# Query stage of a linear-attention layer: one PSUM bank at a time, with its copies in halves and quarters

## The chip, the cores and the metric

The kernel runs on all 8 NeuronCores of one Trainium2 chip. The metric is the device time in microseconds (us) of the slowest core. Every core runs the same program on its own tokens; there is no traffic between cores. Each core has a matrix engine (TensorE, PE in the profile; its weight loads are PEld), a vector engine (VectorE, DVE), an activation engine (ScalarE, ACT), GpSimd (POOL) and a queue engine (SyncE, SP). TensorE writes its results into PSUM, which has 8 banks of 512 f32 columns; VectorE and ScalarE read them from there.

## What is computed

The layer is linear attention, a layer norm, a routed low-rank feed-forward part and a second layer norm. The part around the change is the attention of a query:

```python
q = hidden_states @ Wq.T + bq                 # 16 heads of 128
sq = elu_plus_one(q)                          # elu(q) + 1
kv = jnp.einsum('bhsd,bhse->bhde', sk, v)
qkv = jnp.einsum('bhsd,bhde->bhse', sq, kv)
norm = jnp.einsum('bhsd,bhd->bhs', sq, k_sum)
attn = qkv / (norm[..., None] + EPS)
x = _layernorm(x + attn @ Wo.T)
x = _layernorm(x + ffn(x))
```

The batch has 2 sequences of 8192 tokens and 2048 features. A core owns 2048 tokens of one sequence.

## The kernel before

It has three stages, one after the other.

1. **Keys and values.** 64 tiles of 128 tokens (all of the sequence): lines 281 to 323 on TensorE. The stage ends with `kvb` (the 128x128 matrices kv of 4 key heads) and `ksum_bc`.
2. **Queries.** 16 units of 128 of the core's own tokens, u = 0 to 15. This is the stage that is changed.
3. **Output projection and feed-forward.** Lines 414 to 480 on TensorE, with the weights `wo_t` in the space of the query weights `U0`.

In the query stage two PSUM tensors of 2048 f32 columns (4 banks) alternate: `psQ[0]` is `psA`, `psQ[1]` is `psB`, and unit u uses `psQ[u % 2]` three times over. For a unit TensorE does three groups:

- `q_group(u)` (line 334): 16 steps of `dc` with 4 matmuls each, one to each bank j, so all four banks are filled together and end together; then 4 bias matmuls. 68 matmuls of 512 columns. It waits until `E2` of unit u - 2 has emptied the PSUM tensor (line 340).
- `t_group(u)` (line 355): 16 transposes of 128 columns, from `sqh` into the same PSUM tensor. It waits for `sqhat0` and `sqhat1`.
- `qkv_group(u)` (line 367): 16 matmuls of 128 columns with `kvb`, again into the same PSUM tensor. It waits for `E1`, the copy of the transposes to `sqhT`.

TensorE's order is q(0), q(1), t(0), qkv(0), q(2), t(1), qkv(1), and so on. One turn is q(u), t(u - 1), qkv(u - 1).

VectorE's order in a turn, with the lines of the profile: `min0` of columns 0 to 1023 (547), then for unit u - 1 `E1` (536, the whole 2048 columns to `sqhT`) and `E2` (540, the whole 2048 columns to `sqp`), then `stt0` (552), `min1` of columns 1024 to 2047 (554), `stt1` (557), `prod` (560), `red` (561), three small operations (562, 564, 565), `sqhat0` (568) and `sqhat1` (570). `min0` waits for the end of q(u), `E1` for t(u - 1), `E2` for qkv(u - 1). ScalarE takes the exponential of each `min` (line 651) and `stt0` and `stt1` wait for it. Each operation of VectorE is followed by a wait for its own semaphore (`opq`, line 522).

`sync` stores each `sqp` to `attn_scratch` after `E2` (line 755). GpSimd loads the tokens of two units at a time (`xt_own`, line 727), each load gated by the end of q of an earlier unit (`peq_q`), and after q(15) the eight chunks of `wo_t` (line 739), two in flight at a time, since they overwrite `U0`. The first matmuls of the third stage wait for these chunks.

The dictionaries `peq_*` and `dqabs` at the head of the file hold the semaphore counts of TensorE and VectorE that those waits use.

Of the kernel before, what the change touches and what calls it, by code (L numbers as in the profile page):

```python
# [23 lines left out]
WB_CH = 8  # L24
N_P2W = WO_CH + WB_CH

peq_q, peq_T, peq_qkv = {}, {}, {}
_c = 0
for _u in range(NTC_OWN):
    _c += 1  # L30
    peq_q[_u] = _c
    if _u >= 1:
        _c += 1
        peq_T[_u - 1] = _c
        _c += 1
        peq_qkv[_u - 1] = _c
_c += 1
peq_T[NTC_OWN - 1] = _c
_c += 1
peq_qkv[NTC_OWN - 1] = _c  # L40

pe2_mm3 = {}
pe2_y1t = {}
# [33 lines left out]
def _dq_seg(u, names):  # L77
    global _cq
    for n in names:
        _cq += 1  # L80
        dqabs[(u, n)] = _cq
for _u in range(NTC_OWN):
    _dq_seg(_u, ["min0"])
    if _u >= 1:
        _dq_seg(_u - 1, ["E1", "E2"])
    _dq_seg(_u, ["stt0", "min1", "stt1", "prod", "red", "eps", "recip", "cast",
                 "sqhat0", "sqhat1"])
_dq_seg(NTC_OWN - 1, ["E1", "E2"])
DQ_TOTAL = _cq

_DSEG = {
# [65 lines left out]
def build_nc():  # L157
# [16 lines left out]
    with ExitStack() as ctx:  # L174
# [97 lines left out]
        def slab_wait(eng, g):  # L272
            s = sXTe if g % 2 == 0 else sXTo
            eng.wait_ge(s, 16 * (g // 2 + 1))

        @block.tensor
        def _(tensor):
# [53 lines left out]
            tensor.wait_ge(sWLb, 16 * 12)  # L331
            tensor.wait_ge(sFin, 5)

            def q_group(u):
                par = u % 2
                s_idx = u // 2
                toff = (u - 2 * s_idx) * 128
                slab_wait(tensor, NSLAB_ALL + s_idx)
                if u >= 2:
                    tensor.wait_ge(sDVEq, dqabs[(u - 2, "E2")])  # L340
                for dc in range(16):
                    lhs = slab[s_idx % 2][:, dc, toff:toff + 128]
                    for j in range(4):
                        tensor.matmul(psQ[par][:, j * 512:(j + 1) * 512], lhs,  # L344
                                      U0[:, dc, j * 512:(j + 1) * 512],
                                      start=(dc == 0), stop=False,
                                      skip_group_check=True)
                for j in range(4):
                    mm = tensor.matmul(psQ[par][:, j * 512:(j + 1) * 512],
                                       onesr[:, :],  # L350
                                       rowq[:, j * 512:(j + 1) * 512],
                                       start=False, stop=True, skip_group_check=True)
                mm.then_inc(sPEq, 1)

            def t_group(u):
                par = u % 2
                for h in range(16):
                    if h == 0:
                        tensor.wait_ge(sDVEq, dqabs[(u, "sqhat0")])
                    elif h == 8:  # L360
                        tensor.wait_ge(sDVEq, dqabs[(u, "sqhat1")])
                    mm = tensor.matmul(psQ[par][:, h * 128:(h + 1) * 128],
                                       sqh[:, h * 128:(h + 1) * 128], I_bf[:, :],
                                       start=True, stop=True)
                mm.then_inc(sPEq, 1)

            def qkv_group(u):
                par = u % 2
                tensor.wait_ge(sDVEq, dqabs[(u, "E1")])
                for h in range(16):  # L370
                    mm = tensor.matmul(psQ[par][:, h * 128:(h + 1) * 128],
                                       kvb_v[:, h // 4, :],
                                       sqhT[:, h * 128:(h + 1) * 128],
                                       start=True, stop=True)
                mm.then_inc(sPEq, 1)

            for u in range(NTC_OWN):
                q_group(u)
                if u >= 1:
                    t_group(u - 1)  # L380
                    qkv_group(u - 1)
            t_group(NTC_OWN - 1)
            qkv_group(NTC_OWN - 1)
# [99 lines left out]
        def _(vector):  # L483
# [47 lines left out]
            sqh3 = sqh[:, :].rearrange("p (h d) -> p h d", h=16)  # L531
            rn3 = rnbf[:, :].unsqueeze(2).broadcast_to([128, 16, 128])

            def e1e2(pw):
                vector.wait_ge(sPEq, peq_T[pw])
                opq(vector.tensor_copy(sqhT[:, :], psQ[pw % 2][:, :]))  # L536
                vector.wait_ge(sPEq, peq_qkv[pw])
                if pw >= 1:
                    vector.wait_ge(sSQW, 16 * pw)
                opq(vector.tensor_copy(sqp[pw % 2][:, :], psQ[pw % 2][:, :]))  # L540

            for u in range(NTC_OWN):
                par = u % 2
                vector.wait_ge(sPEq, peq_q[u])
                if u >= 1:
                    vector.wait_ge(sACTq, 2 * u)
                opq(vector.tensor_scalar(scr1[:, :], psQ[par][:, 0:1024], 0.0,  # L547
                                         None, ALU.min))
                if u >= 1:
                    e1e2(u - 1)  # L550
                vector.wait_ge(sACTq, 2 * u + 1)
                opq(vector.scalar_tensor_tensor(sq_p1[:, 0:1024], psQ[par][:, 0:1024],
                                                0.0, scr2[:, :], ALU.max, ALU.add))
                opq(vector.tensor_scalar(scr1[:, :], psQ[par][:, 1024:2048], 0.0,
                                         None, ALU.min))
                vector.wait_ge(sACTq, 2 * u + 2)
                opq(vector.scalar_tensor_tensor(sq_p1[:, 1024:2048],
                                                psQ[par][:, 1024:2048],
                                                0.0, scr2[:, :], ALU.max, ALU.add))
                opq(vector.tensor_tensor(prod3, sq3, ks3, ALU.mult))  # L560
                opq(vector.tensor_reduce(norm16[:, :], prod3, AX.X, ALU.add))
                opq(vector.tensor_scalar(normeps[:, :], norm16[:, :], ATT_EPS,
                                         None, ALU.add))
                opq(vector.reciprocal(rnorm[:, :], normeps[:, :]))
                opq(vector.tensor_copy(rnbf[:, :], rnorm[:, :]))
                if u >= 1:
                    vector.wait_ge(sPEq, peq_T[u - 1])
                opq(vector.tensor_tensor(sqh3[:, 0:8, :], sq3[:, 0:8, :],
                                         rn3[:, 0:8, :], ALU.mult))
                opq(vector.tensor_tensor(sqh3[:, 8:16, :], sq3[:, 8:16, :],  # L570
                                         rn3[:, 8:16, :], ALU.mult))
            e1e2(NTC_OWN - 1)

            dd = [0]

# [109 lines left out]
        def _(gpsimd):  # L685
# [55 lines left out]
            gpsimd.wait_ge(sDVEq, DQ_TOTAL)  # L741
            gpsimd.wait_ge(sACTq, 2 * NTC_OWN)
            gpsimd.wait_ge(sSQW, 16 * NTC_OWN)
            gpsimd.wait_ge(sPEq, peq_T[NTC_OWN - 1])
            for i in range(4, WB_CH):
                gpsimd.dma_start(out=wbase_sb[:, 2 * i:2 * i + 2, :],
                                 in_=wb_src[:, 2 * i:2 * i + 2, :]).then_inc(sWB, 16)
# [3 lines left out]
        @block.sync  # L751
        def _(sync):
            for u in range(NTC_OWN):
                sync.wait_ge(sDVEq, dqabs[(u, "E2")])
                sync.dma_start(out=attn_dram[u], in_=sqp[u % 2][:, :]).then_inc(sSQW, 16)
            def sq_load(u):
                if u < 2:
# [69 lines left out]
```

## Time and profile before

| | us |
|---|---|
| time, median of 2 runs | 1610.43 |
| the two runs | 1610.86, 1610.00 |
| the profiled execution | 1617.76 |
| its span on the slowest core (core 1) | 1616.2 |
| spans of all 8 cores | 1587.3 to 1616.2 |
| TensorE busy on core 1 | 1380.3 (85%) |
| VectorE busy on core 1 | 658.7 (41%) |

The span runs from the first to the last instruction of a core. Start times in rows are us from the start of the span of core 1, the slowest. The key stage fills the time to about 617, the query stage runs from there to 1033, and the third stage from 1054 to the end. The mean granted clock of TensorE over the span is 0.929 of full speed on core 1 and between 0.926 and 0.931 on the others.

### The profile page before, as it was taken

The numbers are of one execution on the slowest core, as the hardware profiler recorded it, in microseconds if no ns is written. First come the engines' busy times: TensorE is split into PE (matmuls) and PEld (weight loads), VectorE is DVE, ScalarE is ACT, GpSimd is POOL, SyncE is SP. The second block draws the span as 40 slices with busy tenths as digits, with TensorE's granted clock in tenths as the row PEclk, the third lists the DMA queues.
The fourth block names the chain that finished last, engine by engine and source line by source line (L and its number), as shares of the span: only waits on it lengthen the run. The fifth ranks groups of instructions, "written<-read, shape, count | busy, mean of one in ns | idle before, by whom it ended". The sixth has DMA issues, their size and how long they took to land.

```text
span 1616.2 us, 16894 instructions; the slowest of 8 cores (1587.3 to 1616.2 us)
## 1 busy us (share of the span) xinstructions
PE 1380.3 (85%) x6808; PEld 615.5 (38%) x6808; DVE 658.7 (41%) x807; ACT 123.1 (8%) x210; POOL 68.8 (4%) x75
## 2 busy tenths in 40 slices
PE   0599999999999988787787877079999999999985
PEld 0244334443444433333333333024444444444432
DVE  0122222222222222656565565424555455545533
ACT  0000000000000000001000010000100010001000
POOL 1000000101000000000000000010000000000000
PEclk9999999999999997788888878589999999999997
DMA  7577875777746523314342021991222113212201
GB/s 111 48 74 82 90 93 78 95 110 93 94 53 71 60 27 52 52 41 78 65 79 52 14 53 27 224 195 49 66 95 101 65 66 102 94 65 71 99 27 53
DMA packets 102894, 123.86 MB, mean 77 GB/s; under 512 B 4384, under 2 KB 86304, under 8 KB 98720
## 3 DMA queue, kind: packets, MB, share of 16 engines
q0 software_dynamic: 93600, 72.43, 34.4%
q1 hardware_dynamic: 6912, 33.56, 5.7%
q10 hardware_dynamic: 2304, 16.78, 3.0%
q8 instruction: 55, 0.90, 0.2%
q14 instruction: 23, 0.19, 0.0%
HBM read 170.02 MB, written 25.17 MB: 121 GB/s over the span
## 4 chain that ended last, share of the span: by engine, by line
PE 77%; DMA 13%; DVE 8%; issue 1%; ACT 0%; DVEq 0%; POOL 0%; POOLq 0%; ACTq 0%
PE psB L463 14%; PE psA L429 13%; PE psA L290 12%; PE psA L293 12%; PE psA L344 8%; DMA u<-xt_full 7%; PE psB L344 7%; DMA u<-wo_t 4%; DVE sqhT L536 2%; DMA sq_p<-brows 2%; PE psB L473 1%; PE psB L468 1%; DVE u L547 1%; PE psA L296 1%; DVE sq_p2b L540 1%
## 5 line engine op out<-in xcount | busy, mean ns | idle before, releaser
L290 PE MATMUL psA<-u 128*128 128x512 bf16 x1024 | 392.6, 383 | 71.3 <-DMA u<-xt_full 68.9
L293 PE MATMUL psA<-u 128*128 128x512 bf16 x1024 | 391.9, 383 | 0.0
L463 PE MATMUL psB<-u,sqhT 128*128 128x512 bf16 x1024 | 235.3, 384 | 0.0
L501 DVE TENSOR_SCALAR u<-psA 128x512 f32<-128x512 f32 x64 | 44.3, 692 | 405.1 <-PE psA L298 405.1
L290 PEld LDWEIGHTS psA<-u 128*128 128x128 bf16 x1024 | 100.8, 98 | 202.0 <-issue 90.5
L429 PE MATMUL psA<-u,sq_p 128*128 128x512 bf16 x512 | 123.2, 389 | 30.4 <-DMA u<-wo_t 27.8
L344 PE MATMUL psA<-u 128*128 128x512 bf16 x512 | 129.8, 421 | 20.9 <-DVE sq_p L540 18.2
L293 PEld LDWEIGHTS psA<-u 128*128 128x128 bf16 x1024 | 101.0, 99 | 115.7 <-issue 4.1
L463 PEld LDWEIGHTS psB<-u,sqhT 128*128 128x128 bf16 x1024 | 100.6, 99 | 115.9 <-issue 5.1
L344 PE MATMUL psB<-u 128*128 128x512 bf16 x512 | 127.6, 416 | 18.3 <-DVE sq_p2b L540 18.3
L429 PE MATMUL psA<-u,sq_p2b 128*128 128x512 bf16 x512 | 120.3, 383 | 2.8 <-DVE fpA L589 2.8
L344 PEld LDWEIGHTS psA<-u 128*128 128x128 bf16 x512 | 53.9, 106 | 96.2 <-issue 48.0
L344 PEld LDWEIGHTS psB<-u 128*128 128x128 bf16 x512 | 53.2, 105 | 90.9 <-issue 41.3
L647 ACT ACTIVATE u<-u 128x512 f32<-128x512 f32 x64 | 40.3, 629 | 559.7 <-DVE u L501 559.7
L429 PEld LDWEIGHTS psA<-u,sq_p 128*128 128x128 bf16 x512 | 49.0, 100 | 84.0 <-issue 37.3
L429 PEld LDWEIGHTS psA<-u,sq_p2b 128*128 128x128 bf16 x512 | 48.8, 99 | 54.2 <-issue 5.9
L505 DVE SCALAR_TENSOR_TENSOR u<-psA,u 128x512 bf16<-128x512 f32 x64 | 44.3, 692 | 57.7 <-ACT u L647 57.7
L651 ACT ACTIVATE u<-u 128x1024 f32<-128x1024 f32 x32 | 33.8, 1056 | 380.4 <-DVE u L547 253.1
L712 POOL DMA_DIRECT2D u<-xt_full x32 | 36.8, 1151 | 519.9 <-PE psA L298 489.0
L672 ACT CAST sqhT<-psB 128x512 bf16<-128x512 f32 x64 | 37.1, 586 | 254.4 <-PE psB L398 254.4
L618 DVE BATCH_NORM_STATS2 bnstB<-fpA 128x6 f32<-128x512 f32 x64 | 44.4, 694 | 7.0 <-DVE bnstB L618 0.5
L595 DVE BATCH_NORM_STATS2 bnstA<-fpA 128x6 f32<-128x512 f32 x64 | 44.4, 694 | 6.6
(109 smaller groups left out, 918.1 us busy)
## 6 DMA issues: line engine op xcount, KB each, us to landing
u<-xt_full POOLq DMA_DIRECT2D x32, 1024.0 KB, 15.1
y<-fpB SPq DMA_DIRECT2D x16, 1024.0 KB, 6.1
u<-wq_t POOLq DMA_DIRECT2D x8, 1024.0 KB, 21.3
u<-xt_own POOLq DMA_DIRECT2D x8, 1024.0 KB, 9.9
u<-wbase_t POOLq DMA_DIRECT2D x8, 1024.0 KB, 16.3
u<-wo_t POOLq DMA_DIRECT2D x8, 1024.0 KB, 16.2
xt_p2a<-x_own ACTq DMA_DIRECT2D x6, 1024.0 KB, 4.9
xt_p2b<-x_own ACTq DMA_DIRECT2D x5, 1024.0 KB, 5.0
```

What stands on the lines that cost most here:

```text
L290: tensor.matmul(psK[par], lhs, wkv_sb[:, dc, 0:512], start=(dc == 0), stop=False, skip_group_check=True)
L293: tensor.matmul(psV[par], lhs, wkv_sb[:, dc, 512:1024], start=(dc == 0), stop=False, skip_group_check=True)
L344: tensor.matmul(psQ[par][:, j * 512:(j + 1) * 512], lhs, U0[:, dc, j * 512:(j + 1) * 512], start=(dc == 0), stop=False, skip_group_check=True)
L429: mm = tensor.matmul(psA[:, j * 512:(j + 1) * 512], sq[:, h * 128:(h + 1) * 128], U0[:, h, j * 512:(j + 1) * 512], start=(h == 0), stop=(h ...
L463: tensor.matmul(psB[:, j * 512:(j + 1) * 512], sqhT[:, dc * 128:(dc + 1) * 128], wbase_sb[:, dc, j * 512:(j + 1) * 512], start=(dc == 0), ...
L501: op(vector.tensor_scalar(scr1[:, 0:512], psK[par], 0.0, None, ALU.min))
L505: op(vector.scalar_tensor_tensor(sk_t[par][:, :], psK[par], 0.0, scr2[:, 0:512], ALU.max, ALU.add))
L595: op2(vector.bn_stats(bnstA[:, g, :], fpA[:, g * 512:(g + 1) * 512]))
L618: op2(vector.bn_stats(bnstB[:, g, :], fpA[:, g * 512:(g + 1) * 512]))
L647: scalar.activation(scr2[:, 0:512], scr1[:, 0:512], AF.Exp).then_inc(sACT1, 1)
L672: scalar.copy(sqhT[:, r * 512:(r + 1) * 512], psB[:, (r % 2) * 512:(r % 2) * 512 + 512]).then_inc(sACT2, 1)
L712: gpsimd.dma_start(out=slab[s % 2], in_=src).then_inc(sXTe if s % 2 == 0 else sXTo, 16)
```

## The change

The query stage is ordered anew; nothing else changes, and the arithmetic is the same.

- **q by banks.** The loop over the banks j is now the outer one: 16 matmuls and the bias matmul fill one bank, then the next. The count of matmuls and of weight loads is the same. Bank j waits only for the quarter `E2c<j>` of unit u - 2. TensorE signals after bank 1 (`peq_qh`) and after bank 3 (`peq_q`).
- **t inside q.** `t_group(u - 1)` is issued between bank 2 and bank 3 of q(u). It signals after 8 and after 16 transposes.
- **E1 in halves.** `E1a` and `E1b`, 1024 columns each. qkv of the first 8 heads waits for `E1a`, of the last 8 for `E1b`.
- **E2 in quarters.** `E2c0` to `E2c3`, 512 columns each; each waits for its 4 heads of qkv.
- **VectorE's order in a turn** is now `min0`, `stt0`, `E1a`, `E1b`, `min1`, `E2c0` to `E2c3`, `stt1`, `prod`, `red`, three small operations, `sqhat0`, `sqhat1`. `min0` waits for bank 1 of q, `min1` for bank 3.
- The wait of `sqhat0` for the transposes of unit u - 1 is left out; the store and the loads wait for the counts that stand in for the old ones.

The diff, with the tables of counts left out:

```diff
@@ tensor @@
-            def q_group(u):
...
-                if u >= 2:
-                    tensor.wait_ge(sDVEq, dqabs[(u - 2, "E2")])
-                for dc in range(16):
-                    lhs = slab[s_idx % 2][:, dc, toff:toff + 128]
-                    for j in range(4):
-                        tensor.matmul(psQ[par][:, j * 512:(j + 1) * 512], lhs,
...
             def t_group(u):
...
-                mm.then_inc(sPEq, 1)
+                    if h == 7 or h == 15:
+                        mm.then_inc(sPEq, 1)
             def qkv_group(u):
                 par = u % 2
-                tensor.wait_ge(sDVEq, dqabs[(u, "E1")])
-                for h in range(16):
+                for i in range(4):
+                    if i == 0:
+                        tensor.wait_ge(sDVEq, dqabs[(u, "E1a")])
+                    elif i == 2:
+                        tensor.wait_ge(sDVEq, dqabs[(u, "E1b")])
+                    for h in range(4 * i, 4 * i + 4):
...
+                    mm.then_inc(sPEq, 1)
             for u in range(NTC_OWN):
-                q_group(u)
...
+                for j in range(4):
+                    if j == 3 and u >= 1:
+                        t_group(u - 1)
+                    if u >= 2:
+                        tensor.wait_ge(sDVEq, dqabs[(u - 2, "E2c%d" % j)])
+                    for dc in range(16):
+                        lhs = slab[s_idx % 2][:, dc, toff:toff + 128]
+                        tensor.matmul(psQ[par][:, j * 512:(j + 1) * 512], lhs,
...
+                    mm = tensor.matmul(psQ[par][:, j * 512:(j + 1) * 512],
+                                       onesr[:, :], rowq[:, j * 512:(j + 1) * 512],
+                                       start=False, stop=True, skip_group_check=True)
+                    if j == 1 or j == 3:
+                        mm.then_inc(sPEq, 1)
                 if u >= 1:
-                    t_group(u - 1)
                     qkv_group(u - 1)
@@ vector @@
+            def e1seg(pw):
+                vector.wait_ge(sPEq, peq_T7[pw])
+                opq(vector.tensor_copy(sqhT[:, 0:1024], psQ[pw % 2][:, 0:1024]))
+                vector.wait_ge(sPEq, peq_T15[pw])
+                opq(vector.tensor_copy(sqhT[:, 1024:2048], psQ[pw % 2][:, 1024:2048]))
+            def e2seg(pw):
+                for i in range(4):
+                    vector.wait_ge(sPEq, peq_qkvq[(pw, i)])
+                    if i == 0 and pw >= 1:
+                        vector.wait_ge(sSQW, 16 * pw)
+                    opq(vector.tensor_copy(sqp[pw % 2][:, i * 512:(i + 1) * 512],
+                                           psQ[pw % 2][:, i * 512:(i + 1) * 512]))
             for u in range(NTC_OWN):
-                vector.wait_ge(sPEq, peq_q[u])
+                vector.wait_ge(sPEq, peq_qh[u])
...
-                if u >= 1:
-                    e1e2(u - 1)
...
+                if u >= 1:
+                    e1seg(u - 1)
+                vector.wait_ge(sPEq, peq_q[u])
                 opq(vector.tensor_scalar(scr1[:, :], psQ[par][:, 1024:2048], 0.0,
                                          None, ALU.min))
+                if u >= 1:
+                    e2seg(u - 1)
...
-                if u >= 1:
-                    vector.wait_ge(sPEq, peq_T[u - 1])
```

## Rows read from the trace of the kernel before

**Rows 1.** Windows by stage: us, engines' busy time (instructions), granted clock, DMA share, GB/s

```profile
650.00:1004.00 354.00, 274.87 (x1400) 128.51 (x1397) 224.62 (x182) 29.58 (x28) 9.76 (x10) 0.84 0.26 51
1004.00:1077.00 73.00, 25.48 (x130) 12.59 (x128) 20.62 (x15) 3.40 (x3) 8.96 (x13) 0.63 0.98 199
1077.00:1616.00 539.00, 509.51 (x2641) 234.96 (x2640) 264.15 (x400) 46.45 (x112) 0.00 (x0) 0.97 0.24 77
```

**Rows 2.** Timeline of TensorE, query stage: start, us, operation, count, idle before it

```profile
709.00 16.89 PE L344 MATMUL psA<-u 128*128 128x512 bf16 x64 [2.61 <-DVE sq_p L540]
...
983.75 1.14 PE L371 MATMUL psB<-sqhT,kvb 128*128 128x128 bf16 x16 [3.01 <-DVE sqhT L536]
987.49 15.89 PE L344 MATMUL psB<-u 128*128 128x512 bf16 x64 [2.61 <-DVE sq_p2b L540]
```

**Rows 3.** Timeline of VectorE in the turn of unit 15

```profile
1004.53 1.23 DVE L547 TENSOR_SCALAR u<-psB 128x1024 f32<-128x1024 f32 x1 [4.62 <-PE psB L349]
1005.92 2.29 DVE L536 CAST sqhT<-psA 128x2048 bf16<-128x2048 f32 x1 [0.17 <-DVE u L547]
1010.33 2.29 DVE L540 CAST sq_p<-psA 128x2048 bf16<-128x2048 f32 x1 [2.11 <-PE psA L371]
1012.79 1.22 DVE L552 SCALAR_TENSOR_TENSOR u<-psB,u 128x1024 bf16<-128x1024 f32 x1 [0.17 <-DVE sq_p L540]
1014.12 1.22 DVE L554 TENSOR_SCALAR u<-psB 128x1024 f32<-128x1024 f32 x1
1016.60 1.22 DVE L557 SCALAR_TENSOR_TENSOR u<-psB,u 128x1024 bf16<-128x1024 f32 x1 [1.25 <-ACT u L651]
...
1022.62 1.22 DVE L568 TENSOR_TENSOR sqh<-u,rnbf 128x1024 bf16<-128x1024 bf16 x1 [0.17 <-DVE rnbf L565]
1023.95 1.23 DVE L570 TENSOR_TENSOR sqh<-u,rnbf 128x1024 bf16<-128x1024 bf16 x1
```

**Rows 4.** Timeline of VectorE, `min0` of unit 0 and of unit 1

```profile
635.13 1.23 DVE L547 TENSOR_SCALAR u<-psA 128x1024 f32<-128x1024 f32 x1 [17.90 <-PE psA L349]
...
650.17 1.23 DVE L547 TENSOR_SCALAR u<-psB 128x1024 f32<-128x1024 f32 x1 [0.24 <-DVE sqh L570]
```

**Rows 5.** One line's instructions (507, key stage): duration ns min/median/max

```profile
L507 DVE CAST u<-psA x64: 690/692/693, 71.3 to 603.3; 128x512 bf16<-128x512 f32 x64
```

**Rows 6.** Timeline of TensorE, units 0 and 1; q(1) follows q(0) without a gap

```profile
617.48 16.57 PE L344 MATMUL psA<-u 128*128 128x512 bf16 x64 [2.65 <-DVE ksum_bc L518]
...
634.95 13.99 PE L344 MATMUL psB<-u 128*128 128x512 bf16 x64
648.87 1.03 PE L349 MATMUL psB<-y1b,onesr 1*128 1x512 bf16 x4
649.83 1.07 PE L362 MATMUL psA<-I_bf,sqh 128*128 128x128 bf16 x16
```

**Rows 7.** Windows in the query stage, columns as in rows 1

```profile
635.00:649.00 14.00, 14.00 (x66) 6.23 (x66) 10.53 (x11) 2.11 (x2) 0.00 (x0) 1.00 0.00 0
882.70:893.10 10.40, 7.79 (x29) 3.31 (x28) 7.25 (x6) 1.06 (x1) 0.00 (x0) 0.53 0.71 128
```

**Rows 8.** Timeline of TensorE, third stage

```profile
1073.62 3.41 PE L429 MATMUL psA<-u,sq_p 128*128 128x512 bf16 x8 [4.08 <-DMA u<-wo_t]
...
1098.13 3.61 PE L429 MATMUL psA<-u,sq_p 128*128 128x512 bf16 x16 [2.61 <-DVE fpA L589]
...
1117.93 3.62 PE L463 MATMUL psB<-u,sqhT 128*128 128x512 bf16 x16
1121.48 0.39 PE L468 MATMUL psB<-sqh,onesr 1*128 1x512 bf16 x1
1121.80 0.39 PE L473 MATMUL psB<-bcat_sb,hmaskT 128*128 128x512 bf16 x1
```

**Rows 9.** Timeline of GpSimd: the first two chunks of `wo_t`

```profile
1004.89 1.41 POOL L739 DMA_DIRECT2D u<-wo_t  x2 [74.12 <-PE psB L349]
```

**Rows 10.** Line 727 (`xt_own`): time from issue to landing

```profile
DMA to landing us min/median/max: 9.6/9.9/14.0
```

## What the change should do to the time

> **What bounds the kernel now.** I read the cores first, then the windows by stage, then the two timelines of one turn side by side, and last the windows of the clock. The spans of the cores differ, but the query stage has the same pattern on those I looked at, so core 1 stands for all. The windows by stage show which part can move: the key stage and the third stage are dense on TensorE (509.5 of 539 us), the query stage is not: 274.9 of 354 us and a granted clock of 0.84 [rows 1]. In the timeline of TensorE the reader is to see two gaps in each turn, 3.01 us before qkv (it waits for `E1`) and 2.61 us before q (it waits for `E2`) [rows 2]. In that of VectorE there are three waits for TensorE: 4.62 us for the end of q, 2.11 us for qkv, and 0.17 us [rows 3]. The two engines take turns: neither is full, and each waits for the other at whole tiles of 2048 columns. From `min0` of unit 1 at 650.17 [rows 4] to `min0` of unit 15 at 1004.53 [rows 3] are 14 turns: 354.4 us, 25.31 us a turn.
>
> A third cost hangs on the gaps. q(1), which has no gap before it, takes 13.99 us for its 64 matmuls [rows 6] at a clock of 1.00 [rows 7], the 2.4 GHz level. q behind the gaps takes 15.89 or 16.89 us [rows 2], since the clock stands at the 1.2 GHz level from about qkv on into q; a stretch of 10.4 us there has a mean of 0.53 [rows 7].
>
> **The change part by part.** The new turn is two chains, and the longer one sets its length. Times within a turn count from the start of `min0`.
>
> VectorE's chain. Start to start, from rows 3: `min0` to `stt0` must now wait for ScalarE, as `min1` to `stt1` does: 1016.60 - 1014.12 = 2.48. Before, `E1` and `E2` lay over that exponential, so this cover is lost. An operation of 1024 columns to the next is 1.33 (1014.12 - 1012.79) without a wait for another engine in front and 1.40 with one (1005.92 - 1004.53). `E1` of 2048 columns is 2.29; a half costs what the operations of 1024 columns on the same PSUM cost, 1.22. So `stt0`, `E1a`, `E1b` are 3 x 1.40 = 4.20, `min1` with two waits behind it 1.47. A quarter of `E2` is a cast of 512 columns from PSUM, 0.69 [rows 5], with 0.17 to the next as behind `min0` (1005.92 less the end of 1004.53 + 1.23, a little rounded up): 0.86, four times 3.44. From `stt1` to `sqhat1` nothing changes: 1023.95 - 1016.60 = 7.35, and `sqhat1` to the next `min0` is 1.23 + 0.24 = 1.47 [rows 4]. The sum is 2.48 + 4.20 + 1.47 + 3.44 + 7.35 + 1.47 = 20.41 us. Without any of the small gaps that I put in front of waits (eight times 0.07) it would be 19.9.
>
> The Trainium skill (VectorE: DVE Perf Modes, The DRAIN you can't avoid) says that a semaphore after each operation costs nothing extra. Rows 3 show 0.07 us more where a wait for another engine stands in front; by the page the chain would be 19.9 us and the time some 7 us lower.
>
> TensorE's chain, from `E2c0` to the next `E2c0`. It sets the turn if the clock and the matmuls are slow. `E2c0` ends 2.48 + 4.20 + 1.47 + 0.69 = 8.84 into a turn. The restart is 0.14 (a copy's end to the first matmul). A bank of 16 matmuls and a bias matmul: by q(1), (649.83 - 634.95) / 4 = 3.72 [rows 6]; by line 463 of the third stage, which already has the bank outside and `dc` inside, 1121.80 - 1117.93 = 3.87 [rows 8]. I take 3.80 and keep both ends. Three banks 11.4, the 16 transposes 0.86 (1.07 less the tail of the last, 0.21) [rows 6], bank 3 another 3.8, its tail and the wakening 0.34, `min1` 1.47 and `E2c0` 0.69. Together 18.7 us at full clock. That is 1.7 less than VectorE's chain, so VectorE becomes the bound. The weight loads do not speak against the new loop: before, each of the 64 matmuls of q had its own too, and line 463 keeps its pace with one each.
>
> What the gaps become. TensorE now ends bank 3 at 8.84 + 0.14 + 11.4 + 0.86 + 3.8 - 20.41 = 4.6 in the next turn. `E1a` ends at 2.48 + 1.40 + 1.22 = 5.10, `E1b` at 6.50, `E2c0` at 8.84. The gaps are about 0.5, 0.9 and 1.6 us with the two halves of qkv (some 0.5 us each) between. Before, they were 3.01 and 2.61. One gap of 2.61 with dense work on both sides left the clock up (16 matmuls in 3.61 us [rows 8]), so the clock should fall in some turns and not in all. What a fall costs is between nothing and 1.9 to 2.9 us (15.89 or 16.89 against 13.99). With 1.7, TensorE's chain is as long as VectorE's: a fall is absorbed, because the delay fills TensorE's own gaps and VectorE does not want bank 3 before `min1` at 6.7. With 2.9 in every turn the chain would be 21.6. I take the turn at 20.4 and keep 19.9 and 21.6.
>
> The waits that are moved. `t_group` now stands in front of bank 3: everything behind it on TensorE waits for `sqhat1`. That ends 1.47 - 1.23 = 0.2 us before the turn's end, at 20.2, and three banks end at 20.4, so it isn't late. The transposes are wanted by `E1a` only at 3.9 of the next turn. Token loads are gated by the end of q as before. A load lands in at most 14.0 us [rows 10], and it is wanted more than a turn (20 us) after its gate. The stores on SyncE's queue have a whole turn.
>
> Start. q(0) ends as before, at 635. `min0` and `stt0` of unit 0 now lie under banks 2 and 3. From `min1` at 635.13 [rows 4] it is 2.48 + 7.35 + 1.47 to `min0` of unit 1: 646.4 in place of 650.17, a gain of 3.7.
>
> End. What follows waits for the end of q(15), because it frees `U0`: the chunks of `wo_t` are issued at 1004.89 [rows 9] and the last one is awaited at 1073.62 [rows 8], 68.7 us in which all other work of the query stage ends as well. These 68.7 us stay as they are and only move. Before, q(15) ended with `min0` of unit 15. Now it ends about 5 us behind it (6.9 if the clock fell): minus 5.6.
>
> The sum: 3.7 + 14 x (25.31 - 20.41) - 5.6 = 3.7 + 68.6 - 5.6 = 66.7 us. The profiled execution took 1617.76, so it would take 1551. It stands 7.3 above the median of the runs, 1610.43, and from that median the forecast is 1543.7, say 1544.
>
> **The rivals.**
>
> A, VectorE's chain bounds the turn: 1544, with 1536 to 1552 as its own range (turn 19.9 to 21.0).
>
> B, the clock falls in every turn as now. For it: the two low stretches of qkv remain between three gaps, and together they last about 4 us. Against it: each gap is half or less of the old ones. TensorE's chain is 21.6, the gain 3.7 + 14 x 3.7 - 7 = 48.5, the time 1562.
>
> C, the gain is given back behind the stage. If the `wo_t` chunks slow down because stores and reloads of `sqp` now fall closer to them, or the third stage finds itself later for its `wbase_t` part, the loss is what the DMA share of 0.98 in that window [rows 1] allows. To come within 2% (32 us) it would have to eat 35 of the 66.7 us. I see nothing that large: the bytes are the same. Time 1578 or more.
>
> D, the other side. TensorE's in-order wait for `sqhat1` in front of bank 3 and the gaps before qkv keep the clock at the 1.2 GHz level through the whole of q. Then a bank takes 17 x 0.427 = 7.3 us (twice a matmul's 0.213 at the upper level), TensorE's chain is 4 x 7.3 + 1.7 + 2.6 = 33.5, and the time is 1610 + 14 x 8.2, about 1725. It decides from a turn of 25.2 us on. Against it: rows 2 and 7 show the clock come back within q each time, after at most 5.8 us of dense matmuls (twice the 2.9 us lost), and the new stretch of dense matmuls is longer.
>
> E, matmuls slower than either row, because the stage is denser. If a bank took 4.7 us in place of line 463's 3.87, TensorE's chain would be 4 x 4.7 + 0.86 + 2.64 = 22.3, the gain 3.7 + 14 x 3.0 - 7 = 38.7, and the time about 1572. The rows speak against it: in q(1), as dense as anything that the change makes, the clock is 1.00 while all eight cores run the same program [rows 7]. The Trainium skill (TensorE: Matmul & The Clock Gate, What's actually happening) has a rule by which this would come: a limit that holds a whole die to 13/16 of the clock once three of its cores run dense matmuls. Rows 7 do not show it.
>
> **How the numbers follow.** A has 0.72, B 0.15, E 0.03, C 0.06 (half of it within 2%), D 0.02, and 0.02 is left for a change that does nothing. A and B together hold more than 8 in 10, so the range runs from below A (1534, for gaps that are smaller than I read them) to B (1562). A measurement of this kernel can tell about 2% from no change, 32 us; that needs a turn of 23 us or less. Faster: 0.93, same 0.04, slower 0.03.
>
> **What would show it.** In the profile after: `min0` to `min0` of 20.4 us with VectorE waiting for TensorE nowhere but a little, 1.25 us of waiting before `stt0` on ScalarE, `min0` of unit 1 at about 646 and of unit 15 at 932, the first `wo_t` issue near 937, gaps before q of 1.6 us or less, a granted clock above 0.9 in the stage, and the third stage of 539 us unchanged. I am wrong if `min1` waits for line 349's successor (TensorE's chain is longer), if q still needs more than 15.5 us in each turn without the transposes, or if the last `wo_t` chunk comes later than 69 us after the first.

## The result, and the profile after

The changed kernel takes 1552.85 us (median of 12 runs) against 1611.01 us (10 runs). The ratio to the kernel before is 0.9628, 95% interval 0.9607 to 0.9650. In a later comparison with more rounds (experiment 11), it was 0.9599 (0.9571 to 0.9627). The profiled execution took 1548.53 us. The forecast was 1544 us, within 1534 to 1562. In some executions of either kernel the cores of one die show a lower granted clock than the others (down to 0.80, against 0.95); the two medians above take them in, without them they are 1549.7 and 1610.9, and all ratios here are without them.

First the windows by stage, core 5, the slowest: the window and its length in us, engines' busy time (instructions) in the order PE, PEld, DVE, ACT, POOL, granted clock, DMA share, GB/s.

```profile
643.00:930.00 287.00, 257.15 (x1402) 116.24 (x1400) 233.64 (x239) 29.59 (x28) 9.76 (x10) 0.96 0.32 63
930.00:1008.00 78.00, 30.56 (x148) 13.72 (x146) 22.04 (x24) 3.40 (x3) 8.94 (x13) 0.65 0.93 186
1008.00:1547.00 539.00, 509.49 (x2640) 234.85 (x2640) 264.22 (x400) 46.39 (x112) 0.00 (x0) 0.97 0.24 77
```

The first row covers 14 turns in 287 us; before, 14 turns took 354 us at a clock of 0.84 [rows 1]. The number of matmuls in it is the same (1402 and 1400). VectorE is busy for 233.6 of 287 us. The third stage is what it was: 539 us and 509.5 of TensorE.

The length of a turn comes from `min0` of unit 1 and of unit 15, and the stage as a whole from its first matmul to the first load of `wo_t`:

```profile
614.84 5.36 PE L386 MATMUL psA<-u 128*128 128x512 bf16 x16 [2.68 <-DVE ksum_bc L533]
...
643.50 1.23 DVE L568 TENSOR_SCALAR u<-psB 128x1024 f32<-128x1024 f32 x1 [0.24 <-DVE sqh L592]
...
930.40 1.23 DVE L568 TENSOR_SCALAR u<-psB 128x1024 f32<-128x1024 f32 x1 [0.24 <-DVE sqh L592]
...
936.02 1.40 POOL L762 DMA_DIRECT2D u<-wo_t  x2 [58.78 <-PE psA L367]
```

A turn is (930.40 - 643.50) / 14 = 20.49 us; before 25.31. The stage up to the `wo_t` load is 936.02 - 614.84 = 321.2 us; before 1004.89 - 617.48 = 387.4 [rows 6, 9]. That is 66.2 us less from slowest core to slowest core. Each core against itself, the stage is 62.1 to 66.4 us shorter. On all eight cores the mean turn lies between 20.47 and 20.54.

One turn of VectorE (start, us, operation, and in brackets the idle time before it and what ended it):

```profile
766.75 1.23 DVE L568 TENSOR_SCALAR u<-psB 128x1024 f32<-128x1024 f32 x1 [0.60 <-DVE sqh L592]
769.23 1.23 DVE L571 SCALAR_TENSOR_TENSOR u<-psB,u 128x1024 bf16<-128x1024 f32 x1 [1.25 <-ACT u L674]
770.62 1.23 DVE L551 CAST sqhT<-psA 128x1024 bf16<-128x1024 f32 x1 [0.17 <-DVE u L571]
772.02 1.22 DVE L553 CAST sqhT<-psA 128x1024 bf16<-128x1024 f32 x1 [0.17 <-DVE sqhT L551]
773.42 1.23 DVE L576 TENSOR_SCALAR u<-psB 128x1024 f32<-128x1024 f32 x1 [0.17 <-DVE sqhT L553]
774.88 0.69 DVE L560 CAST sq_p<-psA 128x512 bf16<-128x512 f32 x1 [0.24 <-DVE u L576]
775.75 0.69 DVE L560 CAST sq_p<-psA 128x512 bf16<-128x512 f32 x1 [0.17 <-DVE sq_p L560]
...
778.34 1.23 DVE L581 SCALAR_TENSOR_TENSOR u<-psB,u 128x1024 bf16<-128x1024 f32 x1 [0.17 <-DVE sq_p L560]
779.67 1.23 DVE L584 TENSOR_TENSOR fpB<-u,ksum_bc 128x2048 bf16<-128x2048 bf16 x1
...
785.64 1.23 DVE L592 TENSOR_TENSOR sqh<-u,rnbf 128x1024 bf16<-128x1024 bf16 x1
787.11 1.23 DVE L568 TENSOR_SCALAR u<-psA 128x1024 f32<-128x1024 f32 x1 [0.24 <-DVE sqh L592]
```

Against rows 3: the waits of 4.62 and 2.11 us for TensorE are gone. What is left is the wait of 1.25 us for ScalarE, which the old order hid, and gaps of 0.17 and 0.24 us. `min0` to `min0` is 20.36 us.

TensorE over the same turn:

```profile
766.63 1.07 PE L353 MATMUL psA<-I_bf,sqh 128*128 128x128 bf16 x16
767.54 3.62 PE L386 MATMUL psB<-u 128*128 128x512 bf16 x16
771.09 0.39 PE L390 MATMUL psB<-y1b,onesr 1*128 1x512 bf16 x1
771.99 0.61 PE L367 MATMUL psA<-sqhT,kvb 128*128 128x128 bf16 x8 [0.52 <-DVE sqhT L551]
773.39 0.61 PE L367 MATMUL psA<-sqhT,kvb 128*128 128x128 bf16 x8 [0.79 <-DVE sqhT L553]
775.72 5.13 PE L386 MATMUL psA<-u 128*128 128x512 bf16 x16 [1.73 <-DVE sq_p L560]
...
781.10 3.63 PE L386 MATMUL psA<-u 128*128 128x512 bf16 x16
...
784.98 3.63 PE L386 MATMUL psA<-u 128*128 128x512 bf16 x16
...
788.86 1.07 PE L353 MATMUL psB<-I_bf,sqh 128*128 128x128 bf16 x16
```

All of its gaps are now waits for VectorE: 0.52, 0.79 and 1.73 us, against 3.01 and 2.61 [rows 2]. In this turn the clock fell (bank 0 takes 5.13 us in place of 3.62), and VectorE's turn above is 20.36 us all the same.

The falls have a pattern that these rows alone do not show. On core 5 bank 0 takes 5.10 to 5.30 us in the turns of units 1, 3, 5 and so on, and 3.61 in those between. A fall makes TensorE 1.5 to 1.7 us late, so in the next turn the copies that qkv waits for are already there: its 16 matmuls run without a gap, only one gap of 1.41 to 1.62 us is left before q, and bank 0 is back at 3.61. Core 1 has the gaps of the rows above in all 14 turns and no fall in any:

```profile
746.53 0.61 PE L367 MATMUL psA<-sqhT,kvb 128*128 128x128 bf16 x8 [0.52 <-DVE sqhT L551]
747.93 0.61 PE L367 MATMUL psA<-sqhT,kvb 128*128 128x128 bf16 x8 [0.79 <-DVE sqhT L553]
750.26 3.61 PE L386 MATMUL psA<-u 128*128 128x512 bf16 x16 [1.73 <-DVE sq_p L560]
```

Core 1, with no fall, has a mean turn of 20.47 us; core 5, with 7, has 20.49; core 3, with 8, has 20.54, the longest. So within one execution the falls cost next to nothing. (In experiment 11 core 1 has falls as well: it is not a property of the core.)

### The profile page after: what moved, and what is told of

The parts are those of the page before. It is cut to its first block, busy times and chain, and to the rows that moved or that the text cites. A ratio compares the mean times of both kernels' runs of the same rounds, so it can differ in the third digit from the quotient of the medians.

```text
span 1547.0 us, 17145 instructions; the slowest of 8 cores (1519.7 to 1547.0 us)
## 1 busy us (share of the span) xinstructions
PE 1365.9 (88%) x6808; PEld 602.6 (39%) x6808; DVE 669.0 (43%) x871; ACT 123.1 (8%) x210; POOL 68.8 (4%) x75
## 4 chain that ended last, share of the span: by engine, by line
PE 67%; DMA 15%; DVE 14%; issue 2%; ACT 1%; DVEq 0%; POOL 0%; ACTq 0%; POOLq 0%
PE psB L478 15%; PE psA L444 14%; PE psA L302 12%; PE psA L305 12%; DMA u<-xt_full 8%; PE psA L386 5%; DMA u<-wo_t 4%; DMA sq_p<-brows 2%; DVE norm L585 2%; PE psB L488 1%; PE psB L483 1%; DVE sq_p2b L560 1%; DVE u L576 1%; PE psA L308 1%; PE psB L421 1%
## 5 line engine op out<-in xcount | busy, mean ns | idle before, releaser
L386 PE MATMUL psB<-u 128*128 128x512 bf16 x512 | 115.9, 379 | 10.4 <-DVE sq_p2b L560 10.4
L386 PEld LDWEIGHTS psB<-u 128*128 128x128 bf16 x512 | 47.9, 98 | 68.1 <-issue 15.3
## 6 DMA issues: line engine op xcount, KB each, us to landing
u<-wq_t POOLq DMA_DIRECT2D x8, 1024.0 KB, 21.3
```

The source lines that it names most:

```text
L386: tensor.matmul(psQ[par][:, j * 512:(j + 1) * 512], lhs, U0[:, dc, j * 512:(j + 1) * 512], start=(dc == 0), stop=False, skip_group_check=True)
```

## The experiments

Two theories stood against each other. Theory 1: VectorE's chain sets the turn, and TensorE has slack in which its work and the falls of the clock disappear. Theory 2: TensorE's chain with its falls of the clock sets it. "Turn" is the mean of 14 turns from `min0` of unit 1 on, in the profile of the slowest core. The ratio is to the kernel before on the same chip. Experiments 1 to 4, 5 to 8 and 9 to 11 ran on three chips, where the medians of the kernel before were 1617, 1612 and 1621 us; so across these groups the ratios are to be compared, not the profiled executions.

| kernel | turn, us | profiled execution, us | ratio (95% interval) |
|---|---|---|---|
| before | 25.31 | 1617.76 | 1 |
| changed | 20.49 | 1548.53 | 0.9628 (0.9607 to 0.9650) |
| 1, one more VectorE operation | 21.84 | 1572.01 | 0.9729 (0.9677 to 0.9781) |
| 2, six more matmuls | 20.47 | 1553.85 | 0.9621 (0.9580 to 0.9662) |
| 3, transposes last | 23.34 | 1602.74 | 0.9895 (0.9856 to 0.9934) |
| 4, whole copies | 20.76 | 1561.61 | 0.9633 (0.9594 to 0.9671) |
| 5, copies in parts only | 24.87 | 1607.33 | 0.9972 (0.9956 to 0.9988) |
| 6, `E1a` over the exponential | 19.55 | 1535.38 | 0.9526 (0.9500 to 0.9553) |
| 7, `E2` on ScalarE | 17.98 | 1509.34 | 0.9369 (0.9341 to 0.9396) |
| 8, both 6 and 7 | 17.57 | 1506.20 | 0.9379 (0.9324 to 0.9434) |
| 9, banks and order only | 25.29 | 1624.38 | 1.0020 (0.9996 to 1.0043) |
| 10, as 8, more rounds | 17.57 | 1512.79 | 0.9342 (0.9313 to 0.9370) |
| 11, changed, more rounds | 20.51 | 1562.19 | 0.9599 (0.9571 to 0.9627) |

**1. One more VectorE operation.**

```diff
                 opq(vector.tensor_tensor(prod3, sq3, ks3, ALU.mult))
+                opq(vector.tensor_tensor(prod3, sq3, ks3, ALU.mult))
```

> The changed kernel with one more VectorE operation in each turn (the product of 2048 columns is done twice, 1.33 us start to start). Theory 1, VectorE's chain sets the turn: the turn grows from 20.4 to 21.8 us, the time by about 20 us to 1571 (15 or 16 operations of 1.33). Theory 2, TensorE's chain with its falls of the clock sets the turn: the operation lies in VectorE's slack, the turn stays within 0.2 us and the time near 1551.

The turn grew by 1.35 us, as theory 1 has it (it is 21.83 or 21.84 on all eight cores), and the profiled execution took 1572 us. By the ratios the time rose by 16 us, with some 9 us to either side, and the turns account for 14 x 1.35 = 19.

**2. Six more matmuls in bank 3.**

```diff
-                    for dc in range(16):
+                    for dc in ([0] * 6 if j == 3 else []) + list(range(16)):
```

> The changed kernel with 6 more matmuls of 512 columns in bank 3 of each unit (the first step is repeated, with no effect on the sum; 1.3 us at the 2.4 GHz level). Theory 1: TensorE has slack of 1.5 us at full clock, so the turn stays at 20.4 to 20.9 us; with 1.3 us each in q(0) and q(15) outside the turns the time is 1553 to 1560. Theory 2: the turn grows by 1.3 us, the time by 20 us to 1571.

The turn stayed at 20.47 us. Two rows of TensorE's timeline show the 22 matmuls of bank 3 and the gap before bank 0, which is still there:

```profile
790.24 4.91 PE L386 MATMUL psA<-u 128*128 128x512 bf16 x22
...
798.07 3.61 PE L386 MATMUL psB<-u 128*128 128x512 bf16 x16 [1.60 <-DVE sq_p2b L560]
```

The added 1.3 us filled the smaller gaps around qkv: in all 14 turns of all eight cores its 16 matmuls now run as one piece. The window over its 14 turns, columns as above:

```profile
646.00:932.00 286.00, 262.62 (x1483) 121.39 (x1481) 233.14 (x238) 29.58 (x28) 9.76 (x10) 1.00 0.32 63
```

The granted clock is 1.00, against 0.96 in the changed kernel. More work on an engine that waits closed two of its gaps, its clock stayed up, and the turn did not grow. Experiments 1 and 2 together show that VectorE's chain sets the turn.

**3. Transposes behind bank 3 again.**

```diff
-                    if j == 3 and u >= 1:
-                        t_group(u - 1)
...
                 if u >= 1:
+                    t_group(u - 1)
                     qkv_group(u - 1)
```

> The changed kernel with the transposes of unit u - 1 back behind bank 3 of q(u). Theory 1: E1a then waits for TensorE, whose chain is 0.14 + 4 banks of 3.87 + 0.65 + E1a, E1b and min1 at 1.40, 1.40, 1.47 + E2c0 0.69 = 21.2 us; the turn is 21.2, the time 11 us above the changed kernel, 1562. Rival: the place of the transposes does not matter, because VectorE has other work then: 1551.

A miss in size: 1602.74 us and a turn of 23.34 us (from 21.3 to 24.2), not 1562 and 21.2. By the ratios it is 43 us above the changed kernel, and the turns account for 14 x 2.85 = 40. One turn, TensorE first and then VectorE:

```profile
871.72 0.61 PE L366 MATMUL psB<-sqhT,kvb 128*128 128x128 bf16 x8 [1.03 <-DVE sqhT L549]
873.12 0.61 PE L366 MATMUL psB<-sqhT,kvb 128*128 128x128 bf16 x8 [0.79 <-DVE sqhT L551]
875.45 6.18 PE L383 MATMUL psB<-u 128*128 128x512 bf16 x16 [1.73 <-DVE sq_p2b L558]
```

```profile
870.35 1.23 DVE L549 CAST sqhT<-psB 128x1024 bf16<-128x1024 f32 x1 [3.34 <-PE psB L352]
```

VectorE waits 3.34 us for the transposes, so TensorE's chain is now the longer one, as expected. Bank 0 takes 6.18 us in place of 3.61: the clock fell, and here 2.57 us a turn have no slack to vanish in. 21.2 + 2.57 = 23.8, which is the length of the later turns. The fall was left out of the expectation. The turn that begins at 699.88 has no fall in front of it, and it is as long as the expectation says (21.31):

```profile
688.50 3.61 PE L383 MATMUL psB<-u 128*128 128x512 bf16 x16 [1.73 <-DVE sq_p2b L558]
```

```profile
699.88 1.23 DVE L566 TENSOR_SCALAR u<-psB 128x1024 f32<-128x1024 f32 x1 [0.24 <-DVE sqh L590]
...
721.19 1.23 DVE L566 TENSOR_SCALAR u<-psA 128x1024 f32<-128x1024 f32 x1 [0.24 <-DVE sqh L590]
```

So of the 2.85 us that this order costs in the mean, 0.8 are the longer chain itself and about 2 the falls that it no longer absorbs. Nor does a late TensorE close the gaps here: all three wait for VectorE's work behind the transposes, so they are back in each turn, and with them the fall (110 of the 112 turns of the eight cores).

**4. Whole copies.**

```diff
-                opq(vector.tensor_copy(sqhT[:, 0:1024], psQ[pw % 2][:, 0:1024]))
-                vector.wait_ge(sPEq, peq_T15[pw])
-                opq(vector.tensor_copy(sqhT[:, 1024:2048], psQ[pw % 2][:, 1024:2048]))
+                vector.wait_ge(sPEq, peq_T15[pw])
+                opq(vector.tensor_copy(sqhT[:, :], psQ[pw % 2][:, :]))
...
-                for i in range(4):
-                    vector.wait_ge(sPEq, peq_qkvq[(pw, i)])
...
+                vector.wait_ge(sPEq, peq_qkvq[(pw, 3)])
+                if pw >= 1:
+                    vector.wait_ge(sSQW, 16 * pw)
+                opq(vector.tensor_copy(sqp[pw % 2][:, :], psQ[pw % 2][:, :]))
...
-                    if u >= 2:
-                        tensor.wait_ge(sDVEq, dqabs[(u - 2, "E2c%d" % j)])
+                    if u >= 2 and j == 0:
+                        tensor.wait_ge(sDVEq, dqabs[(u - 2, "E2")])
```

> The changed kernel with E1 and E2 as one copy of 2048 columns each again; banks, the place of the transposes and VectorE's order stay. Theory 1: VectorE's chain gets shorter (fewer operations), 19.1 us, but bank 0 waits for all of E2, which makes TensorE's chain 20.6 us at full clock; its gap before q grows to 3.1 us, so the clock falls in every turn and costs 1.9 to 2.9: turn 22.5 to 23.5, time 1580 to 1594. Rival, the copies in parts are worth nothing and cost VectorE 1.3 us: turn 19.1 to 20.6, time 1533 to 1553.

The rival was right. The turn is 20.5 us in most turns, TensorE's chain at full clock as computed, and the clock did not fall in each turn. Three rows, TensorE's gap and VectorE's wait:

```profile
783.34 3.61 PE L384 MATMUL psA<-u 128*128 128x512 bf16 x16 [3.01 <-DVE sq_p L555]
```

```profile
758.97 1.23 DVE L570 TENSOR_SCALAR u<-psA 128x1024 f32<-128x1024 f32 x1 [1.48 <-PE psA L388]
...
779.43 1.23 DVE L570 TENSOR_SCALAR u<-psB 128x1024 f32<-128x1024 f32 x1 [1.48 <-PE psB L388]
```

Behind a single gap of 3.01 us, with qkv packed against bank 3, bank 0 still takes 3.61 us. VectorE waits 1.48 us in `min1`: the bound has passed to TensorE, but the copies are 1.3 us cheaper, and the two effects cancel. A few turns were longer, those with or behind a fall of the clock (up to 22.3 us on the slowest core, where bank 0 took 6.25 us); on five of the eight cores the mean turn is 20.46 or 20.47, that of the changed kernel.

**5. Copies in parts only, put into the kernel before.**

```diff
+                vector.wait_ge(sPEq, peq_T7[pw])
+                opq(vector.tensor_copy(sqhT[:, 0:1024], psQ[pw % 2][:, 0:1024]))
                 vector.wait_ge(sPEq, peq_T[pw])
-                opq(vector.tensor_copy(sqhT[:, :], psQ[pw % 2][:, :]))
+                opq(vector.tensor_copy(sqhT[:, 1024:2048], psQ[pw % 2][:, 1024:2048]))
...
-                opq(vector.tensor_copy(sqp[pw % 2][:, :], psQ[pw % 2][:, :]))
+                for i in range(4):
+                    vector.wait_ge(sPEq, peq_qkvq[(pw, i)])
...
+                    opq(vector.tensor_copy(sqp[pw % 2][:, i * 512:(i + 1) * 512],
+                                           psQ[pw % 2][:, i * 512:(i + 1) * 512]))
```

> The kernel before with E1 in halves and E2 in quarters and nothing else: q fills four banks together, t after q, E1 and E2 right behind min0. Theory 1: the parts alone hardly help, since q still starts only after the last quarter: min0 1.40, E1a 1.40, E1b 1.40, four quarters 3.3, restart 0.3, q 14.9 = 22.7 us at full clock, and with the clock falling in each turn (1.9 to 2.9) 24.6 to 25.6 against 25.3: time 1600 to 1614. Rival, the parts are the main thing: turn below 23, time below 1580.

As theory 1 has it: 24.87 us a turn and 0.3% of the time.

**9. Banks and order only: whole copies and transposes last together** (the diffs of 3 and 4).

> The changed kernel with E1 and E2 whole again and the transposes behind bank 3 again: what is left is q by banks and VectorE's order (min0 and stt0 under banks 2 and 3). Theory 1, TensorE's chain: 0.14 + 4 banks of 3.87 + transposes and wakening 1.1 + E1 2.46 + min1 1.47 + E2 2.29 = 22.9 us at full clock; if the clock falls in each turn as it did with the transposes last (2.57 us in bank 0), 25.5, so 1590 to 1620. Rival, order by banks is the part that carries the gain by itself: turn 21 or less, time below 1560.

The turn is 25.29 us, the ratio 1.002: filling q by banks and taking `min0` and `stt0` early gains nothing by itself. TensorE, then VectorE:

```profile
880.84 1.07 PE L352 MATMUL psB<-I_bf,sqh 128*128 128x128 bf16 x16
884.45 1.15 PE L364 MATMUL psB<-sqhT,kvb 128*128 128x128 bf16 x16 [2.54 <-DVE sqhT L547]
888.38 5.43 PE L381 MATMUL psB<-u 128*128 128x512 bf16 x16 [2.79 <-DVE sq_p2b L553]
```

```profile
882.01 2.29 DVE L547 CAST sqhT<-psB 128x2048 bf16<-128x2048 f32 x1 [4.98 <-PE psB L352]
```

The work that VectorE does earlier only moves its wait: it now stands 4.98 us for the transposes instead of 4.62 for the end of q [rows 3]. TensorE's gaps are back at 2.54 and 2.79 us, and the clock falls (0.84 in the stage, as before the change).

Experiments 3, 4 and 9 and the changed kernel are the four corners of a square, all with q by banks and VectorE's new order:

| | transposes behind bank 3 | transposes before bank 3 |
|---|---|---|
| whole copies | 1.002 (25.3 us) | 0.963 (20.8 us) |
| copies in parts | 0.990 (23.3 us) | 0.963, 0.960 (20.5 us) |

The place of the transposes carries the gain, and it needs the banks: without q by banks there is no bank 3 to put them in front of. The copies in parts help in the left column, where TensorE's chain is the longer one and its clock falls in almost every turn, and are about neutral in the right one. VectorE's new order is the same in all four corners; no run takes it back by itself.

**6. `E1a` between `min0` and `stt0`.**

```diff
-    _dq_seg(_u, ["min0", "stt0"])
+    _dq_seg(_u, ["min0"])
     if _u >= 1:
-        _dq_seg(_u - 1, ["E1a", "E1b"])
+        _dq_seg(_u - 1, ["E1a"])
+    _dq_seg(_u, ["stt0"])
+    if _u >= 1:
+        _dq_seg(_u - 1, ["E1b"])
```

> The changed kernel with E1a moved between min0 and stt0, so that it covers the exponential of ScalarE. Theory 1, VectorE's chain sets the turn: it loses the exposed wait, 2.48 + 3 x 1.40 becomes 4 x 1.40: 1.08 us less, 19.3 us; TensorE's chain of 18.9 is then close, and with a fall of the clock longer, so the turn is 19.4 to 20.0 and the time 7 to 15 us below the changed kernel. Theory 2, TensorE's chain sets the turn: no change, within 3 us.

The turn is 19.55 us on the slowest core: 19.3 in most turns, which is VectorE's new chain, and 20.3 and 20.9 in the two behind a fall of the clock (bank 0 at 5.29 and 5.04 us), which no longer fits the slack. By the ratios the time fell by 12 to 16 us against the changed kernel (0.9526 against 0.9599 and 0.9628), where 7 to 15 were expected and the turns explain 14 x 0.94 = 13.

**7. `E2` on ScalarE.**

```diff
-                if u >= 1:
-                    e2seg(u - 1)
...
+            def e2(pw, i):
+                scalar.wait_ge(sPEq, peq_qkvq[(pw, i)])
+                if i == 0 and pw >= 1:
+                    scalar.wait_ge(sSQW, 16 * pw)
+                scalar.copy(sqp[pw % 2][:, i * 512:(i + 1) * 512],
+                            psQ[pw % 2][:, i * 512:(i + 1) * 512]).then_inc(sE2, 1)
```

> The changed kernel with the four quarters of E2 on ScalarE (0.59 us each there) in place of VectorE, ScalarE's order exp of min0, E2c0, E2c1, exp of min1, E2c2, E2c3. Theory 1: VectorE's chain is 2.48 + 3 x 1.40 + 2.48 + 7.35 + 1.47 = 18.0 us, TensorE's is its own work, 17.3 us and a short restart, 17.6; the turn is 18.0 to 18.3, the granted clock close to 1.00 in the stage, the time 1551 - 14 x 2.3 = 1519. Theory 2, the falls of the clock set the turn: less gain, 1530 or more.

The turn is 17.98 us, as computed. VectorE's timeline shows the price of the moved copies: the exponential of `min1` is now exposed as well (the second row, 1.25 us):

```profile
769.45 1.23 DVE L568 TENSOR_SCALAR u<-psA 128x1024 f32<-128x1024 f32 x1 [0.17 <-DVE sqhT L553]
771.93 1.22 DVE L571 SCALAR_TENSOR_TENSOR u<-psA,u 128x1024 bf16<-128x1024 f32 x1 [1.25 <-ACT u L670]
```

By the ratios the time is 37 to 42 us below the changed kernel (0.9369 against 0.9599 and 0.9628), where 32 were expected. The turns account for 14 x 2.5 = 35 of them; the rest is not told apart from the scatter.

**8 and 10. Both edits.**

> Both edits: E2 on ScalarE and E1a between min0 and stt0. Theory 1: VectorE's chain is 16.9 us, so TensorE's own work (4 banks of 3.87, transposes 0.86, qkv 0.9 and a restart of 0.3) sets the turn at 17.5 us; the time is 7 us below the kernel with E2 on ScalarE alone, 1512. Rival, ScalarE or a wait for it becomes the bound: no gain over E2 on ScalarE alone.

> The kernel with E2 on ScalarE and E1a between min0 and stt0 once more, with more rounds. The turn in its profile was 17.57 us against 17.98 without the second edit, so 14 x 0.41 = 6 us less: 1504, ratio 0.933 to the kernel before. If the two are alike in time, ratio 0.937.

The turn is 17.57 us. One row of TensorE and two of VectorE:

```profile
770.72 3.61 PE L388 MATMUL psB<-u 128*128 128x512 bf16 x16 [0.21 <-ACT sq_p2b L672]
```

```profile
765.40 1.23 DVE L554 CAST sqhT<-psB 128x1024 bf16<-128x1024 f32 x1 [0.95 <-PE psB L355]
...
769.62 1.23 DVE L575 TENSOR_SCALAR u<-psA 128x1024 f32<-128x1024 f32 x1 [0.20 <-PE psA L392]
```

TensorE's gap before q is 0.21 us, and VectorE waits for TensorE: the bound is TensorE's own work, 17.5 us (it is busy for 242.3 of 245 us in the stage). In time the second edit isn't shown to add anything: experiment 7 gives 0.9369 (0.9341 to 0.9396), 8 gives 0.9379 and 10 gives 0.9342, and the intervals overlap. The 6 us that the turns show are too few to be told from the scatter. The kernels of 7 and 8 are the fastest of the study; in the comparison of 10 with 11, on the same chip, that is 2.7% below the changed one (0.9342 against 0.9599).

**11. The changed kernel again.**

> The changed kernel once more on the same chip as the two others, with more rounds. The stage itself got 66 us shorter on each core (the prediction's sum was 66.7); the ratio 0.9628 says 60. If the ratio here is 0.959, all of the stage's gain arrives; if it is 0.963 again, some 6 us are given back outside the stage.

0.9599 lies nearer to the first case, 0.959. Its interval ends at 0.9627, just under the second, and overlaps that of the first comparison (0.9607 to 0.9650), so the two are not told apart. The premise was too neat: core by core the stage gained 62.1 to 66.4 us, not 66 on each. So a part of the difference between 60 and 66 may lie within the stage itself, and whether the time gains 60 or 65 us stays within what the runs can tell.

## Why the prediction was right

- **Turns before.** Both engines waited for each other at whole tiles. Right: experiment 9, which keeps whole tiles in another order, has the same turn (25.29 us) and the same clock (0.84).
- **VectorE's chain, 20.41 us.** Measured 20.36 in a turn, 20.47 to 20.54 in the mean. Each term came out: `min0` to `stt0` 2.48, then 1.39, 1.40, 1.40, 1.46, quarters at 0.87, `stt1` to `sqhat1` 7.30 (forecast 7.35: `sqhat0` no longer waits for the transposes), and 1.47 to the next `min0`. The longer turns (20.7) have an extra gap of 0.3 to 0.4 us between two VectorE operations with no other engine behind it, as the 0.60 us in the first row of VectorE's timeline above.
- **The small gaps in front of waits.** The prediction put 0.07 us before each wait for another engine, from rows 3. The profile after has 0.17 us there, and 0.24 where two waits stand, against 0.10 between operations without such a wait (778.34 + 1.23 to 779.67). Without them the chain would be 19.9 us, which is not what this trace shows. What the Trainium skill states (VectorE: DVE Perf Modes, The DRAIN you can't avoid) is that a semaphore behind each VectorE operation costs nothing extra. It does not speak of waits for other engines, to which the prediction stretched it, and no run here tests what it does state.
- **TensorE's chain.** The bank was 3.88 us (781.10 to 784.98) at the upper clock, so of the two ends the one from line 463 [rows 8] was right; the prediction took 3.80. That makes the chain 19.0 us and its slack 1.4, not 1.7. With the whole `E2`, 2.29 in place of 0.69, it would be 20.6; experiment 4, where this chain is the bound, gives 20.5 and so checks the sum.
- **A sign of being wrong that did show, in small.** "I am wrong if `min1` waits for line 349's successor": that is line 390, and `min1` waits for it in some turns. A fall of 1.7 us is a little more than the slack. On core 5 `min1` stands still for 0.20 to 0.33 us in three turns in place of 0.17, on core 3 for 0.38 in five. That is at most 1.1 us in the whole stage, so VectorE's chain is the bound by a margin that the falls just use up.

```profile
752.72 1.22 DVE L576 TENSOR_SCALAR u<-psA 128x1024 f32<-128x1024 f32 x1 [0.33 <-PE psA L390]
```

- **Gaps and clock.** The gaps were forecast at 0.5, 0.9 and 1.6 us and were 0.52, 0.79 and 1.73 in the turn shown; in most others the first is 0.17, and behind a fall the first two are closed. The clock fell in some turns only (every second one on core 5, none on core 1), the mean is 0.96 and not the 0.84 of before, and the falls were absorbed. Rival B did not occur. How often the clock would fall was a guess: the prediction's ground, smaller gaps, holds on core 1 and on core 5 alike, and only one of them has falls.
- **Start and end.** The stage began 2.6 us earlier than before, at 614.84, so the forecast times of 646, 932 and 937 came as 643.5, 930.4 and 936.0. From the first matmul of the stage to `min0` of unit 1 it is 643.50 - 614.84 = 28.7 us, against 650.17 - 617.48 = 32.7 before [rows 4, 6]: a gain of 4.0, forecast 3.7. The load of `wo_t` came 5.62 us after `min0` of unit 15 (7.2 or 7.3 on three cores, 4, 6 and 7), forecast 5.6. From that load to the matmuls that wait for its last chunk it was 68.7 us on the slowest core, as before, and 64.7 to 69.8 over all cores, before 64.9 to 70.1: it only moved. Rivals C, D and E did not occur: the third stage takes 539 us as before, and the turn is shorter than 25.2 and 22.3 us. (The limit of the Trainium skill that the prediction names under E stands on that page under Seeing it yourself. At 0.96 the profiled execution does not show it.)
- **The sum.** 66.7 us forecast for the stage, 66.2 from slowest core to slowest core, 62.1 to 66.4 core by core, 60 to 65 in the ratios. So 1544 is 5.7 us below the median of 1549.7; a part of that may be that the sum was worked out for core 1 alone, while cores 4, 6 and 7 gained only 62.1 to 62.9. The profiled pair differs by 69.2. The key stage in front of the change scatters by more than these differences: the query stage of the changed kernel began at 614.8 us on the slowest core here and at 624.0 in experiment 11. No run separates the rest.

What the prediction did not say, and the runs did, is which part mattered. It priced the parts as one chain. Without the transposes before bank 3 nearly all of the gain is gone (1.002 with whole copies, 0.990 with parts); without the copies in parts it stays (0.963).

Two expectations of the experiments were wrong, both on the clock. In 3 I left out the fall, and it came in each later turn and cost 2.57 us. In 4 I put it in, and it came in few. What tells them apart in the rows: in 4 the gap is one piece of 3.01 us between dense work; in 3 the gaps of 1.03, 0.79 and 1.73 us have only two pieces of qkv of 0.6 us between them. The changed kernel bears this out in part: on seven cores 46 of the 48 turns with the gaps in front of both halves of qkv have a fall, and 43 of the 50 without them have none. But core 1 has these gaps in all 14 turns and never a fall, so the pattern alone does not settle it. Why a given turn or core is hit stays open.

## What to carry to other kernels

When two engines take turns on the same tiles, write both of them out as a chain from one point of a turn to the same point of the next, with start-to-start times from the trace, and find for each hand-over who stands behind it in order; the edit that pays is the one that takes a hand-over out of the longer chain (here 16 transposes, moved one bank ahead), not the one that makes all pieces smaller. Then look which chain is the longer one and move its work to the engine that idles: the four copies on ScalarE gave another 2.4 to 2.7% (0.9369 against 0.9599 and 0.9628). An added operation on each engine in turn, 1.3 us here, tells in two runs which chain sets the time. And slack is worth having beyond the mean: here a fall of the clock cost next to nothing where TensorE had 1.4 us to spare and about 2 us a turn where it had none.

## What the runs showed of the hardware

- Six more matmuls a unit raised the mean granted clock of the stage from 0.96 to 1.00 and left the turn as it was (20.47 us against 20.49). Here it was waiting, not work, that lowered this clock.
- A single gap of 3.01 us left the clock at 2.4 GHz in most turns of experiment 4. Three gaps with 3.55 us in sum and two short pieces of work between them lowered it in each later turn of experiment 3 (bank 0: 6.18 us in place of 3.61). Three gaps with 2.7 to 3.0 us in sum lowered it in 46 of 48 such turns on seven cores of the changed kernel and in none of 14 on core 1.
- In PSUM an f32 cast of 512 columns took VectorE 0.69 us and a cast of 1024 columns 1.22 us, against 2.29 for 2048: four quarters with their gaps are 3.46 us (774.88 to 778.34), one whole copy 2.46 (1010.33 to 1012.79 in rows 3).
